# Interleaved token tiles for dt and u, and u B products issued among decay products of other row tiles, in a selective-scan stage on one core

## The reference

```
xs, z = split(h @ in_w);  xs = silu(xs);  proj = xs @ xproj_w
dt = softplus(proj[..., :512] + dt_bias)
B, C = proj[..., 512:576], proj[..., 576:]
A = -exp(A_log)
for each token t:
    state = state * exp(dt[t][:, None] * A) + (dt[t] * xs[t])[:, None] * B[t][None, :]
    y[t] = sum over the 64 states of state * C[t]
y = y + xs * D
```

## Time and profile before

| | |
|---|---|
| median of three runs | 8568.34 us |
| profiled execution | 8568.23 us, span 8566.4 us |
| TensorE busy | 8058.2 us |
| ScalarE busy | 4793.8 us |
| VectorE busy | 4216.2 us |
| GpSimd busy | 3326.1 us |
| mean granted clock of TensorE | 0.668 |

### The profile page before, as it was taken

The page is one execution under the profiler, slowest core; times in us unless marked ns, Lnnn a source line. Parts: engine busy times, 40 slices in busy tenths (PEclk is TensorE's granted clock), DMA queues, the critical chain, the costliest instruction groups (busy, mean ns, idle before and its releaser), DMA issues. The chain is left out here.

```text
span 8566.4 us, 182764 instructions
## 1 busy us (share of the span) xinstructions
PE 8058.2 (94%) x68920; PEld 4046.4 (47%) x68920; DVE 4216.2 (49%) x6974; ACT 4793.8 (56%) x9618; POOL 3326.1 (39%) x2814
## 2 busy tenths in 40 slices
PE   7887899999999999999999999999988999997898
PEld 3443444444444444444444454544433555544444
DVE  3445355555455555545555555555543444435554
ACT  3555566666666666666666666666512443435554
POOL 0111344444444444444444444544501322323333
PEclk8998555555555555555555555555589999999999
DMA  6666111111111111111111111111162000000000
GB/s 177 166 155 156 48 44 42 42 43 40 48 41 44 42 42 43 45 42 41 44 42 42 49 40 42 43 42 42 33 233 90 8 8 8 8 4 33 11 11 8
DMA packets 781155, 458.64 MB, mean 54 GB/s; under 512 B 646848, under 2 KB 701760, under 8 KB 762112
## 3 DMA queue, kind: packets, MB, share of 16 engines
q1 hardware_dynamic: 777184, 445.32, 18.4%
q10 hardware_dynamic: 3104, 1.57, 0.1%
HBM read 301.29 MB, written 145.49 MB: 52 GB/s over the span
## 5 line engine op out<-in xcount | busy, mean ns | idle before, releaser
L1409 POOL TENSOR_TENSOR s_dec<-s_hs,s_dec 128x512 f32<-128x512 f32 x2040 | 2550.2, 1274 | 2609.6 <-DVE s_hs L1449 1790.2
L1339 ACT ACTIVATE s_dec<-s_pa 128x512 f32<-128x512 f32 x4096 | 2223.3, 594 | 838.0 <-PE s_pa L1228 838.0
L1228 PE MATMUL s_pa<-s_dl,s_al 18*128 18x64 bf16 x32768 | 2521.5, 281 | 107.8 <-ACT s_dec L1339 50.2
L1228 PEld LDWEIGHTS s_pa<-s_dl,s_al 18*128 18x128 bf16 x32768 | 1866.5, 115 | 1047.8 <-ACT s_dec L1339 845.7
L1263 PE MATMUL s_py<-s_hs,s_cz 128*32 128x256 f32 x16384 | 2198.4, 634 | 0.0
L1438 DVE TENSOR_TENSOR s_pA<-s_pA,s_dec 128x512 f32<-128x512 f32 x2040 | 1405.2, 695 | 1251.4 <-ACT s_hs L1345 841.7
L1449 DVE TENSOR_TENSOR s_hs<-s_pB,s_dec 128x512 f32<-128x512 f32 x2040 | 1325.1, 686 | 1243.0 <-PE s_py L1263 1168.5
L1345 ACT COPY s_hs<-s_pA 128x512 f32<-128x512 f32 x2048 | 1208.3, 590 | 1024.2 <-PE s_pA L1239 1024.2
L1239 PE MATMUL s_pA<-az 18*128 18x256 bf16 x4096 | 1229.3, 402 | 9.1 <-issue 1.6
L1239 PE MATMUL s_pB<-az 18*128 18x256 bf16 x4096 | 1192.2, 401 | 0.0
L1263 PEld LDWEIGHTS s_py<-s_hs,s_cz 128*32 128x32 f32 x16384 | 424.2, 141 | 745.1 <-issue 517.4
(11 more groups left out here) (254 smaller groups left out, 5681.3 us busy)
## 6 DMA issues: line engine op xcount, KB each, us to landing
s_dl<-D SPq DMA_DIRECT2D x512, 144.0 KB
az<-U SPq DMA_DIRECT2D x1024, 72.0 KB
az<-B SPq DMA_DIRECT2D x1024, 36.0 KB
D<-p_dp SPq DMA_DIRECT2D x128, 192.0 KB, 4.1
U<-p_up SPq DMA_DIRECT2D x30, 768.0 KB, 6.6
B<-p_bz SPq DMA_DIRECT2D x144, 128.0 KB, 2.5
SZ<-p_sz SPq DMA_DIRECT2D x16, 1024.0 KB, 3.9
SK<-p_skip SPq DMA_DIRECT2D x16, 1024.0 KB, 5.7
```

Source lines behind the costliest of these rows:

```text
L1228: mm = pe.matmul(pa[:, banks[e], DS * i:DS * (i + 1)], al[QR * q:QR * q + ROWS, d, :], dl[w[0]][QR * q:QR * q + ROWS].rearrange("p t i d - ...
L1339: act.activation(dec[w][:].rearrange("p t i d -> p (t i) d")[:, :, DS * q + d:DS * q + d + 8], pa[:, bank, :].rearrange("p (d c) -> p c d" ...
L1409: pool.tensor_tensor(m, two(hs[k][:, (x + 1) % 2, :]), m, ALU.mult).then_inc(m_done, 1)
```

## The change

1. dt and u are kept in four interleaved token tiles: tile q holds tokens 4 f + q. In `prepare`, `tokens` picks every fourth token of xs as the stationary operand; `pre`, `soft`, `dt` have the token tile as their innermost index; `u`, `ur`, `dp`, `up` are rearranged. D in DRAM then has four tokens innermost, and is stored by 4 DMAs for each unit and direction; U is stored by 4.
2. In the scan `dl` is [P, 2 * UNITS, DS, 4]: the 64 moving columns of a decay product are 16 runs of four bf16 elements, 8 bytes. `dec` is laid out to match, so that a chunk of a token is two runs of 256 elements.
3. The operands of the u B products of chunk k go to row tile RG[k], RG = (2, 3, 0, 1). The two pA products of chunk 0 are issued before the first and the fourth pair of the decay products w = 0 (row tiles 0 and 1), those of pB for chunk 2 likewise in w = 1 (row tiles 2 and 3). Their waits move with them, and the wait of y on `c_filled` at x = 2 is dropped.
4. A in DRAM is addressed flat, with its 18 rows in a new order; sizes are the same.

```diff
-    return {"D": flat("D3", "r m i j b c d t").rearrange("(s q a t i d) -> s q a t i d", s=4, q=4, t=T, i=UNITS, d=TS),
-            "U": flat("U3", "r m i j b c t d").rearrange("(s k a t v d) -> s k a t v d", s=4, k=4, t=T, v=2, d=D),
+    return {"D": flat("D3", "r m i j b c d t").rearrange("(s a q k i f) -> s a q k i f", s=4, q=4, k=TS, i=UNITS, f=D),
+            "U": flat("U3", "r m i j b c t d").rearrange("(s c a k v f) -> s c a k v f", s=4, c=4, k=TS, v=2, f=4 * D),
             "B": flat("B3", "r i m j b c t f").rearrange("(r k a t v f) -> r k a t v f", r=2, k=4, t=T, v=2, f=P),
+            "A": flat("A3", "n m j b d f").rearrange("(n a d f) -> n a d f", n=2 * IC, d=P, f=P),
             "Yt": flat("Y", "r m i p b t").rearrange("(m p a t) -> m p a t", m=2 * IC, p=P, t=T)}
+
+
+def tokens(tile, k, q):
+
+    return tile[:, k, :].rearrange("p (f q) -> p q f", q=4)[:, q]
+
+
+def halves(tile):
+
+    return tile[:].rearrange("p (h d) q -> p h (d q)", h=2)
+
+
+def by_half(tile):
+
+    return tile[:].rearrange("p h q d -> p h (q d)")
...
-        pre = sb("pre", [P, 4, DI])
-        sp_ = sb("soft", [P, 4, DI])
-        dt_ = sb("dt", [P, 4, DI])
-        u = sb("u", [P, 4, DI])
-        ur = sb("ur", [P, 4, DI])
-        dp = sb("dp", [P, PARTS, 4, DI], BF16)
-        up = sb("up", [P, PARTS, 4, DI], BF16)
+        pre = sb("pre", [P, DI, 4])
+        sp_ = sb("soft", [P, DI, 4])
+        dt_ = sb("dt", [P, DI, 4])
+        u = sb("u", [P, 2, 4, D])
+        ur = sb("ur", [P, 2, 4, D])
+        dp = sb("dp", [P, 2, PARTS, 4 * D], BF16)
+        up = sb("up", [P, 2, PARTS, 4 * D], BF16)
...
-                    for m in range(IC):
-                        for h in range(2):
-                            at = P * m + TS * h
-                            sp.dma_start(scratch["D"][2 * r + m // 2, 2 * (m % 2) + h, :, :, i].rearrange(
-                                "a (k p) d -> p (a k) d", p=P),
-                                         dp[:, :, :, at:at + TS].rearrange("p j k d -> p (j k) d")
-                                         ).then_inc(s["dp_out"], 16)
+                    for half in range(2):
+                        for b in range(PAIR):
+                            sp.dma_start(scratch["D"][2 * r + half, PARTS * b:PARTS * b + PARTS, :, :, i].rearrange(
+                                "j q k f -> k (j q) f"),
+                                dp[P // 2 * b:P // 2 * (b + 1), half].rearrange("p j (q f) -> p (j q) f", q=4)
+                                ).then_inc(s["dp_out"], 16)
 
                 def store_u(i, r):
                     wait(sp, s["up2"], 2 * i + r + 1)
                     for half in range(2):
-                        sp.dma_start(scratch["U"][2 * r + half, i // 2, :, :, i % 2].rearrange(
-                            "a (k p) d -> p (a k) d", p=P),
-                            up[:, :, :, half * D:(half + 1) * D].rearrange("p j k d -> p (j k) d")
-                            ).then_inc(s["up_out"], 16)
...
-                            mm = pe.matmul(g0[:, q, :], xs[r][:, k, q * P:(q + 1) * P], xp_w[r][:, k, 0:DI],
+                            mm = pe.matmul(g0[:, q, :], tokens(xs[r], k, q), xp_w[r][:, k, 0:DI],
...
-                        mm = pe.transpose(g1[:, q % 2, m * P:(m + 1) * P], xs[r][:, m, q * P:(q + 1) * P], ident[:])
+                        mm = pe.transpose(g1[:, q % 2, m * P:(m + 1) * P], tokens(xs[r], m, q), ident[:])
...
-                        dve.tensor_tensor(pre[:, q, :], g0[:, q, :], dtbb[:, r, :], ALU.add
+                        dve.tensor_tensor(pre[:, :, q], g0[:, q, :], dtbb[:, r, :], ALU.add
...
-                        dve.tensor_tensor(u[:, q, :], g1[:, q % 2, :], dt_[:, q, :], ALU.mult).then_inc(s["u_done"], 1)
+                        dve.tensor_tensor(u[:, :, q, :], g1[:, q % 2, :].rearrange("p (h d) -> p h d", h=2),
+                                          dt_[:].rearrange("p (h d) q -> p h d q", h=2)[:, :, :, q], ALU.mult).then_inc(s["u_done"], 1)
...
+    RG = (2, 3, 0, 1)
...
-        dec = [sb(f"dec{e}", [P, TB, UNITS, HALF]) for e in range(2)]
+        dec = [sb(f"dec{e}", [P, 2, UNITS, TU, HALF]) for e in range(2)]
...
-        dl = [sb(f"dl{e}", [P, TB, UNITS, DS], BF16) for e in range(2)]
+        dl = [sb(f"dl{e}", [P, 2 * UNITS, DS, TU], BF16) for e in range(2)]
...
-            return dec[x // TB % 2][:, x % TB, 2 * k:2 * k + 2, :]
+            return dec[x // TB % 2][:, x // TU % 2, 2 * k:2 * k + 2, x % TU, :]
...
-                        rows = scratch["D"][s, q, :, k * TB:(k + 1) * TB].rearrange("a t i d -> a (t i d)")
-                        sp.dma_start(dl[k % 2][QR * q:QR * q + ROWS].rearrange("p t i d -> p (t i d)"),
+                        rows = scratch["D"][s, :, q, 2 * k:2 * k + 2].rearrange("a k i f -> a (k i f)")
+                        sp.dma_start(dl[k % 2][QR * q:QR * q + ROWS].rearrange("p i d t -> p (i d t)"),
...
+                        r = QR * RG[k]
+                        rows = scratch["U"][s, k, :, j].rearrange("a v f -> a (v f)")
+                        sp.dma_start(ul[j % 2][r:r + ROWS].rearrange("p v t d -> p (v t d)"),
...
-                def adt(p, w, banks):
-
+                def adt(p, w, banks, beside=None):
+
+                    if beside:
+                        beside(0)
                     wait(pe, taken, 2 * p - 1)
                     for i in range(8):
+                        if beside and i == 3:
+                            beside(1)
                         for e in range(2):
                             q, d = 2 * (w[1] % 2) + e, 8 * (w[1] // 2) + i
                             mm = pe.matmul(pa[:, banks[e], DS * i:DS * (i + 1)],
                                            al[QR * q:QR * q + ROWS, d, :],
-                                           dl[w[0]][QR * q:QR * q + ROWS].rearrange("p t i d -> p (t i) d")[:, :, d],
+                                           dl[w[0]][QR * q:QR * q + ROWS, :, d, :],
                                            start=True, stop=True)
                     mm.then_inc(filled, 1)
 
-                def bu(out, k, x, first, signal):
+                def bu(out, k, x, v, first, signal):
 
                     j, t = x // TU, x % TU
-                    r = slice(QR * k, QR * k + ROWS)
-                    for v in range(2):
-                        mm = pe.matmul(out[:, HALF * v:HALF * (v + 1)], bl[j % 2][r, t, v, :], ul[j % 2][r, t, v, :],
-                                       start=first, stop=True, skip_group_check=not first)
-                    mm.then_inc(signal, 1)
-
-                def to_a(n, x, k):
-                    wait(pe, mul, 2 * n + k + 1)
-                    bu(pA[:, k, :], k, x, False, bu_a)
-
-                def to_b(n, x, G, k):
-
-                    if k == 2 and x % TU == 0:
+                    r = slice(QR * RG[k], QR * RG[k] + ROWS)
+                    mm = pe.matmul(out[:, HALF * v:HALF * (v + 1)], bl[j % 2][r, t, v, :], ul[j % 2][r, v, t, :],
+                                   start=first, stop=True, skip_group_check=not first)
+                    if v:
+                        mm.then_inc(signal, 1)
+
+                def to_a(n, x, k, v):
+                    if v == 0:
+                        wait(pe, mul, 2 * n + k + 1)
+                    bu(pA[:, k, :], k, x, v, False, bu_a)
+
+                def to_b(n, x, G, k, v):
+
+                    if k == 2 and v == 0 and x % TU == 0:
                         uses = 2 * G + x // (2 * TU) + 1
                         wait(pe, u_in[x // TU % 2], UQ * uses)
                         wait(pe, b_in[x // TU % 2], BQ * uses)
-                    wait(pe, added, 2 * n - 3 + k)
-                    bu(pB[:, k - 2, :], k, x, True, bu_b)
+                    if v == 0:
+                        wait(pe, added, 2 * n - 3 + k)
+                    bu(pB[:, k - 2, :], k, x, v, True, bu_b)
...
                         late = x == 1
                         before = (x - 1) % BODY
                         has = not (head and x == 0)
-                        to_a(n, x, 0)
+                        ahead = not (last and x == BODY - 1)
+
+                        def to_a0(v):
+                            to_a(n, x, 0, v)
+
+                        def to_b2(v):
+                            to_b(n + 1, (x + 1) % BODY, G + (x + 1) // BODY, 2, v)
+
                         if more:
-                            produce(G, x, 0, head, turn)
-                        to_a(n, x, 1)
+                            produce(G, x, 0, head, turn, to_a0)
+                        else:
+                            to_a0(0)
+                            to_a0(1)
+                        for v in range(2):
+                            to_a(n, x, 1, v)
                         if has and not late:
-                            if x == 2:
-                                wait(pe, c_filled, 2 * G + 1)
                             if x == 9:
                                 wait(pe, c_filled, 2 * G + 2)
```

(14 more changed lines are left out.)

60 lines of the change are left out of this document (31 added, 29 removed).

## The result

The changed kernel takes 7392.41 us, median of four runs (7387.62 to 7394.92), against 8567.33 (8566.32 to 8568.66) for the kernel before: a ratio of 0.8628, 95% interval 0.8613 to 0.8643. The forecast's direction was right, its size was not: 843 us were predicted.

A forecast was written before the change was run, and what follows sets the result against it. The prediction took TensorE to bound the scan: 8568.2 us less 850 in the scan, plus 12 in the preparation, less 7 for stores, gave 7723, stated as 7725, range 7620 to 7870; with rivals and preparation's ends, 7480 to 8150.

The forecast's parts named there:

- The pair's spacing s: Scan: time per pair of decay products on two row tiles, forecast to fall from 0.110 to 0.080 us.
- second rival: Scan: pairs take only their columns, 0.053 us; w = 1 stretch 0.64, w = 0 1.15; 7515 us; chance 0.22 with clock.
- 0.59 at x = 0 and 8: Scan, tokens where the other half of dec must be complete: 0.59 us saved at each, VectorE's multiply being late.
- steady at 0.90: Scan, steady token: 0.66 us saved with w = 1 and 0.25 with w = 0, taken as 0.90, 4.94 to 4.04.
- x = 1 at 0.5: Scan, token x = 1 of each body, where y comes later: 0.5 us counted as saved.
- The clock: Whole kernel: TensorE's granted clock could rise from 0.50; given 3 in 100, within the case of s = 0.053.
- +12: Preparation: 12 us added for strided weight loads of xs and VectorE's strided pre and dt; range end +80.
- The stores' -7: Preparation's end: fewer D stores with longer runs save 7 us, an estimate between 0 and -14.
- The mechanism in both stretches: Scan, decay product stretches: runs of four shorten pairs; u B products on other row tiles overlap them; 1.40 to 0.74, 1.50 to 1.25.
- 0.98 and 1.41: Scan: w = 1 and w = 0 stretches if runs bring nothing, s = 0.110; total 8115 us, chance 0.25.
- rival 4: Scan: ScalarE's ring of copies and exp sets the token at 4.4 us; about 8090 us, chance 0.08.
- rival 3: Scan: the queue lets nothing past, w = 0 stretch 1.84 us for 1.50; slower, 8890 us, chance 0.05.

The follow-up runs named there:

- e10: Changed kernel with VectorE's preparation in plain rows and ScalarE copying dt once per half unit into the interleaved order; 7377.48 us, ratio 0.8610.
- e1: Changed kernel with the u B products back on their old row tiles and places, runs of four tokens kept; 7850.75 us, ratio 0.9163.
- e2: Kernel before with only the new placement of u B products, old layout of dt and u; 7995.81 us, ratio 0.9333.
- e3: Changed kernel with the same product order, but u B products on their old row tiles; 7920.91 us, ratio 0.9244.

## Why the prediction was wrong

**The pair's spacing s is the step that failed.** The text took 0.080 us, 40 ns taken off 0.110, plus 0.010 because a weight load "may be only partly covered". The 40 ns were a good reading of the records (46 ns measured), but a spacing is not a record: the stretch with w = 1 is 0.54 us for eight pairs, so with a drain of 0.11 a pair is 0.054. The spacing fell by 56 ns where the record fell by 46. The better step was at hand. If a decay product's record is longer by the time that its reads need, then the 120 ns between its record and a u B product's, with 256 columns (0.213 us), give 0.213 - 0.120 = 0.093 for a distant read of 64 columns; that is 40 ns over the 0.053 of the columns, so an adjacent read has only the columns left, with nothing added. The records after bear this out: 399 less 235 is 164 ns, and 192 columns at 1.2 GHz are 160. (Why distant products follow each other in 0.110 and not in 0.093 stays open.) The addition for the weight load had no row behind it, and the text had just shown that a load's record is not what it occupies. The rows after show that again: twelve loads begin and end in 0.40 us on two tiles, each recorded at 120 ns. The Trainium skill, "TensorE: Matmul & The Clock Gate", section on LDWEIGHTS, has P / 1.2 ns for a load of P columns, 107 for 128. As a bound on how closely loads follow one another on a row tile the trace does not bear it out, since a pair, with one load on each tile, passes every 0.053 us.

With s = 0.053 the text's own second rival has 0.64 and 1.15 us for the stretches, a token of 3.83 and a total of 7515 (7520 by its own terms). Measured are 0.54, 1.18 and 3.74. The 0.64 counted an interleaved pB pair that ends last; the rows show it let past, ending with the decay products. The 1.15 was right to 0.03, and for the reason given: the pair of k = 1 is let past a few decay products only, starts 0.64 us into the stretch (the forecast had 0.72 with its slower pairs) and ends it.

**The other tokens of a body were under-sized.** The text had 0.59 at x = 0 and 8, from 0.24 ahead of the multiply and 0.35 behind it; measured are 0.73 at x = 0 and 0.83 at x = 8, there 0.35 ahead and 0.47 behind. It counted x = 2 and x = 3 as steady at 0.90 and x = 1 at 0.5, 2.3 us for the three; they gave 3.99. So a body fell by 18.6 us, not 13.4, and not by rival 2's 16.6 either. Of the 5.2 us that the forecast missed in a body, 3.2 are the eleven steady tokens (1.19 for 0.90), 1.7 the three behind x = 0, and 0.4 the two at x = 0 and 8. Why the three tokens behind x = 0 gained more than their own stretches was not tried apart; that stays open.

**The clock** had 3 chances in 100 to rise, on the rows of the last tokens. It rose for 72 us of the scan, worth about 24 us; no rival had a price for so small a part.

**The preparation was mis-sized: +5 predicted, +34 measured.** For VectorE the text had bounds of 0 and double (0 to 87 us), and took +12 for it and the weight loads together because exp's writes of dec, "also strided", cost nothing. That was the wrong neighbour: those writes go in runs of eight adjacent float32 numbers, while pre and dt take single ones, 16 bytes apart. The copy of e10, which writes single numbers 16 bytes apart on exp's own engine, lasts 3.91 us where a plain pass takes 1.90. The rule of the Trainium skill, "SBUF — State Buffer", section "Door 1: The DMA port swizzle" (note on cachelines), that the text used for the decay products speaks against this part of the change too, and was not held against it: four bytes in every sixteen is one hit a line. The same note of the Trainium skill lists a stride of 4 float32 numbers as free; the trace does not agree (682 to 1076 ns), and the measurement decides. The bounds held, the value in them did not. The stores' -7 came to about -2 where it can be read.

**What was right.** The mechanism in both stretches: e1 and e2 give them one by one, and e2's two stretches are the text's 0.98 and 1.41 to 0.01. That products on different tiles overlap, and that order alone gains nothing (e3). That the placement gives nothing at x = 8, where VectorE is late (4.87 us with and without, once the layout is there; without the layout it gives 0.48). That ScalarE's exp stays covered, near 80% busy, so rival 4 did not come; and rival 3, a queue that lets nothing past, did not either. Rival 2 had 0.22 and should have had more than the forecast, for the two reasons that the text itself gave for it: the u B products' rate in the earlier trace rows and the Trainium skill's rule on lines of 16 bytes, named above.

The sizes close: the scan gave 1214.7 us where 850 were predicted, 365 more (the clock's 24 among them), and the preparation took 34 where 5 were predicted, 29 back. 365 - 29 is the 336 by which the sum of 7723 stands over the profiled run's 7387.62.
